# Decoder layer on one core: the first cross-attention batch loaded in 256 KB pieces, and self attention's loads and stores issued by ScalarE

## The reference

```python
x = x + self_attention(layernorm(x))       # 16 heads of 32, causal, biases
x = x + cross_attention(layernorm(x), ctx) # 16 query heads of 128 on 8 key/value heads; ctx is 64 tokens of 256, mask over them
x = x + experts(layernorm(x))              # 8 experts of rank 64; each token takes the expert of its largest logit
```

## Time and profile before

| | us |
|---|---|
| median of 3 runs | 1533.86 (1533.47 to 1535.66) |
| profiled execution | 1535.35 |
| its span, first to last instruction | 1533.6 |
| TensorE busy | 1382.5 (90% of the span) |
| VectorE / GpSimd / ScalarE busy | 1092.7 / 757.2 / 729.9 |
| mean granted TensorE clock | 0.966 |

### The profile page before, as it was taken

One profiled execution on the slowest core, in us unless ns is written; L12 is line 12 of the kernel. 1 busy time (PEld: TensorE's weight loads), 2 busy tenths in 40 slices (PEclk: granted clock), 3 DMA queues, 4 the chain that ended last, 5 costly groups with the idle time before them and its releaser, 6 DMA issues.

```text
span 1533.6 us, 28325 instructions
## 1 busy us (share of the span) xinstructions
PE 1382.5 (90%) x10592; PEld 1140.9 (74%) x10592; DVE 1092.7 (71%) x2037; ACT 729.9 (48%) x1739; POOL 757.2 (49%) x570
## 2 busy tenths in 40 slices
PE   7878778999998999999995778999999999999998
PEld 5656667777787877777874567888888887888886
DVE  4336486777878787877775577878787877787865
ACT  5444567666676667676674432323232323232221
POOL 2321266767777676867675643334343433343310
PEclk9999989999999999999998789999999999999999
DMA  8999587879898979888888731313130313030000
GB/s 321 306 316 292 118 153 135 166 159 160 169 162 160 164 141 182 162 168 168 155 145 232 189 144 47 116 34 125 30 138 28 133 33 132 28 136 30 28 15 28
DMA packets 378872, 212.57 MB, mean 139 GB/s; under 512 B 337648, under 2 KB 337776, under 8 KB 375024
## 3 DMA queue, kind: packets, MB, share of 16 engines
q1 hardware_dynamic: 378736, 210.74, 57.1%
HBM read 76.49 MB, written 50.33 MB: 83 GB/s over the span
## 4 chain that ended last, share of the span: by engine, by line
PE 48%; DVE 26%; issue 5%; ACT 4%; DMA 4%; POOL 2%; SPq 0%; DVEq 0%; ACTq 0%; POOLq 0%
PE banks L44 35%; DVE a_neg_max L803 4%; PE banks L936 4%; PE banks L1535 3%; DMA a_turned<-shared 3%; DVE b_xn L1378 2%; PE banks L970 2%; DVE a_y_sum L822 2%; DVE shared L812 2%; ACT a_probs L706 2%; PE banks L944 2%; DVE b_probs L1427 1%; PE banks L971 1%; DVE b_row_sum L1432 1%; DVE b_row_max L1425 1%
## 5 line engine op out<-in xcount | busy, mean ns | idle before, releaser
L626 POOL TENSOR_TENSOR shared<-a_probs,shared 128x768 f16<-128x768 f32 (+1 forms) x192 | 349.4, 1820 | 204.9 <-DVE shared L812 183.0
L706 ACT ACTIVATE a_probs<-banks,a_neg_max 128x128 f32<-128x128 f32 (+3 forms) x512 | 265.1, 531 | 210.9 <-DVE a_neg_max L803 184.0
L803 DVE TENSOR_REDUCE a_neg_max<-banks 128x2 f32<-128x256 f32 (+3 forms) x256 | 203.7, 818 | 115.4 <-PE banks L944 114.7
L1231 POOL TENSOR_TENSOR b_probs<-b_probs,b_row_scale 128x1024 f32<-128x1024 f32 x32 | 61.0, 1907 | 200.8 <-DVE b_row_scale L1437 200.8
L970 PE MATMUL banks<-a_v,a_turned 128*128 128x96 bf16 x1280 | 123.5, 212 | 32.3 <-DMA a_turned<-shared 25.8
L970 PEld LDWEIGHTS banks<-a_v,a_turned 128*128 128x128 f16 x1280 | 99.8, 100 | 65.5 <-issue 34.5
L1212 POOL TENSOR_TENSOR b_rstd<-b_var,b_minus_half 128x1 f32<-128x1 f32 x64 | 35.3, 551 | 189.4 <-DVE b_var L1373 189.4
L1304 ACT ACTIVATE b_probs<-b_probs 128x1024 f32<-128x1024 f32 x32 | 33.9, 1059 | 182.2 <-DVE b_probs L1427 182.2
L971 PE MATMUL banks<-a_v,a_turned 128*128 128x64 bf16 x1280 | 119.3, 196 | 0.0
L44 PE MATMUL banks<-a_xt_hi,w_qkv_hi 128*128 128x512 f32 x256 | 110.5, 432 | 6.5 <-DVE a_yt_lo L777 4.7
L706 ACT ACTIVATION_READ_ACCUMULATOR a_probs<-banks,a_neg_max 128x1 f32 x512 | 105.9, 207 | 0.0
(11 more groups left out here) (172 smaller groups left out, 3983.2 us busy)
## 6 DMA issues: line engine op xcount, KB each, us to landing
m_dram<-c_m_out SPq DMA_DIRECT2D x8, 2048.0 KB, 13.7
vw_dram<-shared SPq DMA_DIRECT2D x32, 512.0 KB, 8.3
b_vw_raw<-vw_dram SPq DMA_DIRECT2D x8, 2048.0 KB, 8.0
shared<-m_dram SPq DMA_DIRECT2D x7, 2048.0 KB, 8.4
c_w_raw<-w_group_dram SPq DMA_DIRECT2D x7, 1280.0 KB, 11.5
a_x_res<-x_dram SPq DMA_DIRECT2D x32, 256.0 KB, 3.5
x_dram<-a_x_res SPq DMA_DIRECT2D x32, 256.0 KB, 2.9
b_x<-x_dram SPq DMA_DIRECT2D x32, 256.0 KB, 2.7
```

Source lines behind the costliest of these rows:

```text
L626: nc.gpsimd.tensor_tensor(part(u, 1), probs[:, u % PROB_SLOTS, 0:2 * columns_of(u // 2)], part(u, 0), ALU.subtract).then_inc(parts_ready, 1)
L706: ins = nc.scalar.activation(probs[:, u % PROB_SLOTS, to:to + width], score[:, j, at:at + width], ACT.Exp, bias=neg_max[:, c:c + 1], accum ...
L803: ins = nc.vector.tensor_reduce(neg_max[:, c:c + 2], score[:, 2 * half:2 * half + 2, at:at + width], AX, ALU.max, negate=True)
L1231: nc.gpsimd.tensor_tensor(probs[:, :, :], probs[:, :, :], row_scale[:, :].unsqueeze(2).to_broadcast([P, XH, S]), ALU.mult).then_inc(probs_ ...
```

## The change

Three things are done. In self attention ScalarE issues `load_x`, `load_x_res` and `store_x1` at the end of its round, and SyncE's loop keeps only the transposes; the residual of the last batch is loaded by SyncE after the last transposes (`LAST_X_RES_AT` one round later), and the last four stores stay with SyncE. The loads of the first cross-attention batch are cut into 256 KB pieces: eight for M, one a round in rounds 84 to 91, into two buffers that lie where xn was and in free space; x1 tiles 0 and 1 and the mask in round 92; VW's first two pieces in round 94, all by ScalarE; VW's other six and x1 tiles 2 and 3 by SyncE after the last transposes. The head of the next stage is woven in earlier and shared differently: M is split by ScalarE in rounds 93 and 94, its low parts are made by GpSimd in rounds 94 and 95 and by VectorE at the end of round 95 and after it; three of VW's four low parts go from GpSimd to VectorE; the split of the expert weights moves behind tile 1's exponentials; and for tiles 2 and 3 TensorE makes its scores ahead of `turn_probs` of the tile before.

```diff
-    LAST_X_RES_AT = B * NR - 1
+    LAST_X_RES_AT = B * NR
...
+        INPUTS_FREE_AT = (B - 1) * NR
...
@@ self attention, sync
             for r in range(B * NR + 1):
                 for u in units_of(r - 1):
                     turn_parts(u)
-                for use in FILLED[2 * r - 2] + FILLED[2 * r - 1] if r else []:
-                    if use[1] == "o":
-                        store_x1(use[0], [use[2]])
-                if r in X_AT:
-                    load_x(*X_AT[r])
-                if r in X_RES_AT:
-                    load_x_res(*X_RES_AT[r])
                 if r == LAST_X_RES_AT:
                     for t in range(TT):
-                        load_x_res(B - 1, t)
-                if r == WEIGHTS_FREE_AT:
-
-                    sp.wait_ge(gemm_full, PROJECTED)
-                    sp.wait_ge(x1_stored, TT * 16)
-                    sp.wait_ge(vw_stored, XG * 64 + 64)
-                    next(then)
+                        load_last_x_res(B - 1, t)
+
+            sp.wait_ge(vw_stored, XG * 64 + 64)
+            next(then)
@@ self attention, gpsimd
-                if r == B * NR - 2:
+                if r in (B * NR - 2, B * NR - 1, B * NR):
                     next(then)
-                if r == B * NR:
-                    pool.wait_ge(parts_ready, 2 * B * NR)
-                    next(then)
-                if r == B * NR + 1:
-                    next(then)
+            pool.wait_ge(parts_ready, 2 * B * NR)
             next(then, None)
@@ self attention, scalar: the end of a round
-            next(then)
+                for use in FILLED[2 * r - 2] + FILLED[2 * r - 1] if r else []:
+                    if use[1] == "o":
+                        store_x1(use[0], use[2])
+                if r in X_AT:
+                    load_x(*X_AT[r])
+                if r in X_RES_AT:
+                    load_x_res(*X_RES_AT[r])
+                if r == INPUTS_FREE_AT:
+                    act.wait_ge(gemm_drained, drained((B - 1, "xt", KT - 1)))
+                if INPUTS_FREE_AT <= r < INPUTS_FREE_AT + XG:
+                    next(then)
+                if r == WEIGHTS_FREE_AT:
+                    act.wait_ge(gemm_full, PROJECTED)
+                    act.wait_ge(x1_stored, TT * 16)
+                if r >= WEIGHTS_FREE_AT:
+                    next(then)
@@ cross attention, sync
-        for t in range(TT):
-            load_x1((0, t, t))
-        sp.dma_start(mask_u8[:, :], mask.to_broadcast([P, B * S])).then_inc(small_loaded, 16)
-        sp.dma_start(m_first[:, :], m_dram[0].rearrange("p g m -> p (g m)")).then_inc(m_first_loaded, 16)
-        load_vw(0)
+        for g in range(2, XG):
+            load_vw_first(g)
+        load_x1((0, 2, 2))
+        load_x1((0, 3, 3))
         yield
         load_m(1)
-        sp.wait_ge(vw_lo_by_pool, len(VW_POOL))
-        sp.wait_ge(vw_lo_by_dve, len(VW_DVE))
+        sp.wait_ge(vw_first_lo_ready, CHUNKS)
@@ cross attention, gpsimd
-            if second:
-                we_low(0)
             if is_tile(b):
                 scale_probs(b * TT + t)
...
             if second:
+                we_low(0)
                 we_low(2)
...
         deviation(2, 0)
-        yield
         m_low(0, 0, 0)
+        yield
         m_low(0, 2, 0)
+        yield
         deviation(2, 1)
         yield
         vw_low(0, 0)
-        vw_low(0, 2)
-        yield
-        vw_low(0, 3)
@@ cross attention, scalar (in step, the split of the expert weights and that tile's split_m move behind the xt2 copy)
-        act.wait_ge(m_first_loaded, 16)
-        for c in range(CHUNKS):
-            split_m(0, c, 0)
+        for g in range(XG):
+            nc.scalar.dma_start(m_first[g // HALF][:, g % HALF, :], m_dram[0, :, g, :]).then_inc(m_first_loaded, 16)
+            yield
+        for t in range(2):
+            nc.scalar.dma_start(x1[:, t, :], x1_dram[0, t * P:(t + 1) * P, :]).then_inc(x1_loaded[t], 16)
+        nc.scalar.dma_start(mask_u8[:, :], mask.to_broadcast([P, B * S])).then_inc(small_loaded, 16)
+        yield
+        act.wait_ge(m_first_loaded, XG * 16)
+        split_m(0, 0, 0)
+        split_m(0, 1, 0)
+        yield
+        split_m(0, 2, 0)
+        split_m(0, 3, 0)
+        for g in range(2):
+            nc.scalar.dma_start(vw_raw[:, g * D:(g + 1) * D], vw_dram[0, :, g, :]).then_inc(vw_first_loaded, 16)
+        yield
         yield
         copy_hi(flat(xt2_hi), turn[0][:, :], xt2_full, 1, xt2_hi_ready)
         for c in range(CHUNKS):
             split_vw(0, c)
         copy_hi(flat(xt2_hi), turn[0][:, :], xt2_full, 2, xt2_hi_ready)
@@ cross attention, vector
+        m_low(1)
         normalise(2, x1[:, 0, :], 0)
         yield
-        m_low(1)
         m_low(3)
...
-        for c in VW_DVE:
+        for c in range(1, CHUNKS):
             vw_low(0, c)
@@ cross attention, tensor (step)
+            lead = isinstance(here, int) and 1 < here < TT
+            if lead:
+                make_scores(b, t, here, par)
             if done and not second:
-                turn_probs(done[2], here is not None)
+                turn_probs(done[2], here is not None and not lead)
...
-            if here is not None and not second:
+            if here is not None and not second and not lead:
                 make_scores(b, t, here, par)
```

More of the change, by code:

```diff
@@ L715, in parts_hi, with load_x, load_x_res, store_x1 @@
                 nc.scalar.activation(part(u, 0), probs[:, u % PROB_SLOTS, 0:2 * columns_of(u // 2)], ACT.Copy).then_inc(hi_by_act, 1)
+            def load_x(b, t):
+                if t == 0:
+                    act.wait_ge(gemm_drained, drained((b - 1, "xt", KT - 1)))
+                nc.scalar.dma_start(xn[:, t, :], x[b, t * P:(t + 1) * P, :]).then_inc(x_loaded[t], 16)
+            def load_x_res(b, t):
+                if b and t == 0:
+                    act.wait_ge(x1_stored, b * TT * 16)
+                nc.scalar.dma_start(x_res[:, t, :], x[b, t * P:(t + 1) * P, :]).then_inc(x_res_loaded[t], 16)
+            def store_x1(b, t):
+                act.wait_ge(gemm_drained, drained((b, "o", t)))
+                nc.scalar.dma_start(x1_dram[b, t * P:(t + 1) * P, :], x_res[:, t, :]).then_inc(x1_stored, 16)
             for use in AHEAD:
@@ L1014 @@
 PLACE = {
-    "m1_lo": 17536, "m0_hi": 33920, "m0_lo": 50304, "vw_raw": 66688, "xt2_hi": 84096, "xt2_lo": 86144, "xn2": 88192, "mask_u8": 90240,
-    "m_first": 91776, "pt_hi": 91776, "pt_lo": 95872, "probs": 99968, "xn3": 104064, "hidden": 106112,
+    "m1_lo": 17536, "m0_hi": 33920, "m0_lo": 50304, "vw_raw": 66688,
+    "m_first0": 83072, "probs": 84096, "hidden": 88192,
+    "x1": 91776, "xt2_hi": 99968, "xt2_lo": 102016, "xn2": 104064, "mask_u8": 106112, "xn3": 106112,
     "m1_hi": 108160, "vw_hi": 124544, "we_hi": 140928, "we_lo": 158336, "x2": 175744, "xt3_hi": 183936, "mask_add": 186496, "mask_f": 188544,
-    "vw_lo": 190592, "xt3_lo": 206976, "ht_hi": 209024, "ht_lo": 211072, "x1": 219712, "small": 227904, "end": 229368,
+    "vw_lo": 190592, "xt3_lo": 206976, "ht_hi": 209024, "ht_lo": 211072,
+    "m_first1": 219776, "pt_hi": 219776, "pt_lo": 223872, "small": 227968, "end": 229368,
 }
@@ L1052, in cross_attention_and_experts @@
     vw_raw = at("vw_raw", PLACE["vw_raw"], [P, KT * EW], F32)
-    m_first = at("m_first", PLACE["m_first"], [P, MW], F32)
+    m_first = [at(f"m_first{n}", PLACE[f"m_first{n}"], [P, HALF, KT * 2 * S], F32) for n in range(2)]
     m_hi, m_lo = ([at(f"m{p}_{n}", PLACE[f"m{p}_{n}"], [P, MW], F32R) for p in range(2)] for n in ("hi", "lo"))
@@ L1154, in is_second, with m_source @@
         return isinstance(n, int) and n == 1
+    def m_source(b, c):
+        if is_first(b):
+            return m_first[c // 2][:, c % 2 * 2:c % 2 * 2 + 2, :].rearrange("p g m -> p (g m)")
+        return m_raw[:, chunk(c)]
     def m_lo_count(b):
@@ L1263, in gpsimd @@
         deviation(2, 0)
+        m_low(0, 0, 0)
         yield
-        m_low(0, 0, 0)
         m_low(0, 2, 0)
+        yield
         deviation(2, 1)
@@ L1287, in split_m @@
                     act.wait_ge(score_full, (b - 1) * TT)
[L1288 to L1289 removed]
+            nc.scalar.activation(m_hi[par][:, chunk(c)], m_source(b, c), ACT.Copy).then_inc(m_hi_ready, 1)
         def split_vw(b, c):
[L1292 to L1293 removed]
+            if c == 0 and is_first(b):
+                act.wait_ge(vw_first_loaded, XG * 16)
+            elif c == 0:
+                act.wait_ge(vw_loaded, b * 16)
             if not (isinstance(b, int) and b == 0):
@@ L1317, in step @@
                 copy_hi(flat(xt3_hi), turn[2][:, :], xt3_full, gated[2] + 1, xt3_hi_ready)
-            if second:
-                act.wait_ge(we_loaded, 16)
-                for k in range(KT):
-                    nc.scalar.activation(we_hi[:, k, :], vw_raw[:, expert_rows(k)], ACT.Copy).then_inc(we_hi_ready, 1)
-            if is_tile(b) and is_tile(b + 1):
+            if is_tile(b) and is_tile(b + 1) and not second:
                 for c in M_BESIDE[t]:
@@ L1334, in step @@
```

(6 more changed lines are left out.)

32 lines of the change are left out of this document (14 added, 18 removed).

## The result

The kernel after took 1539.88 us (median of 12 runs), the kernel before 1534.57 beside it: ratio 1.0041, 95% interval 1.0025 to 1.0057, so some 6 us slower. Forecast was 1524.0, in 1514 to 1532, with a chance of 0.80 for faster. The profiled execution of after took 1539.42 us with a span of 1537.6, 4.0 over the span of before.

The account below looks back on a forecast made before the run. TensorE bounds both stages; their handover stalls on transposes queued behind 5 MB. Gains of 13.7, then 14.4, fell to 8.3 at VW, ended at 9.3, about 10 with the clock; self attention 0: 1535.35 to 1525.4 profiled, 1524 median, range 1514 to 1532.

Parts of the forecast that it names:

- The stall: Handover, round 95's scores: transposes no longer stand behind 5 MB, so scores start at 835.5 instead of 849.2, gain 13.7 us.
- VW's six pieces: Handover, before tile 1's scores: VW lands at about 862, tile 1 starts at 869.0, gain down to 8.3 us.
- Behind tile 1's scores: Later handover: TensorE no longer waits for GpSimd behind its VW low parts, about +1 us.
- The expert split: Handover: moving it behind the exponentials gives 0, since VectorE's row subtraction ended as late as ScalarE's split.
- The lead: Handover, tiles 2 and 3: scores ahead of `turn_probs`, bounds +2 to -3 us, taken as 0.
- The x1 tile behind VW: Handover: SyncE still issues batch 1's VW ahead of the next x1 tile, so that wait stays.
- clock's return: End of the handover: TensorE's clock returning adds a little, taking the gain from 9.3 to about 10 us.
- Self attention, taken as 0: Rounds 0 to 91: loads and stores issued by ScalarE lie in its gaps; bounds -5 and +8 us, cost 0.
- (a): Handover: VW's pieces land one after another, the last at 880, tile 1 18 us later: 1542 us; chance 0.03.
- (b): Self attention, rounds with two issues: ScalarE held 2.0 us an issue, 28 us in all, 1552 us; chance 0.06.
- (c): Handover: VW lands at 868, or GpSimd's and VectorE's low parts hold each other: 1531 us; chance 0.17.
- (d): Handover: the VW wait does not appear and VectorE drops its contention, 14.4 us stay: 1517 us; chance 0.14.

Follow-up runs that it names:

- the run with the burst on ScalarE: Kernel before, with round 92's 5 MB (x1, mask, M, VW) issued in whole loads by ScalarE at the round's end instead of by SyncE: ratio 0.9982.
- VW by ScalarE: Kernel after, with VW's pieces 2 to 7 issued by ScalarE at the end of round 95 instead of by SyncE behind the residual loads: ratio 0.9976.
- combined: Kernel after, ScalarE issuing VW's pieces 2 to 7, tiles 2 and 3's scores behind turn_probs, expert-weight split put back, batch 1's first x1 before its VW: 1522.29 us.
- issues-only runs: Kernel before, with only self attention's x loads, residual loads and x1 stores (rounds 0 to 91) moved from SyncE to ScalarE, run twice: ratios 1.0018 and 1.0012.

## Why the prediction was wrong, point by point

The forecast was a gain of 10 us for the profiled execution, and it lost 4.0. Of these 14.0 us, 6.0 stand ahead of tile 1's scores (gain forecast 8.3, measured 2.3) and 8.0 behind them (forecast 1.7 more, measured 6.3 less).

*The stall: right in place, 1.5 us too large, and by the wrong cause.* Round 95 started at 836.98, forecast 835.5. The text put the stall down to the transposes' place behind 5 MB in SyncE's queue. The run with the burst on ScalarE shows that the place made 3.5 us of it and the 5 MB in flight 12.3. The forecast came near because the change took away both, and that is luck: by the same working a burst moved whole to another queue would have been given the same gain. The change helped because those bytes no longer flow at once. That they came in pieces is not enough: where ScalarE issues VW's last six pieces, 1.5 MB, together beside the last transposes, TensorE's waits for these between 836 and 862 us are 5.1 us (VW by ScalarE) and 9.1 (combined), in after 0.2:

```profile
PE banks L980 <- DMA a_turned<-shared: 5.1, 2, 4.0
...
PE banks L980 <- DMA a_turned<-shared: 9.1, 3, 4.5
```

All 5 MB in pieces at once were not tried. What remains of the bytes has its price by the same cause: the 12.2 us are 15.8 less in round 94, 1.3 more in round 93 beside the x1 and mask loads (7.1 to 7.6 us in all kernels made from after, 6.1 in before), 1.2 more in rounds 84 to 92 beside M's pieces, and 1.1 from ahead of these.

*VW's six pieces: the first failed term.* Forecast was VW at 862 and tile 1 at 869.0, a gain left of 8.3 us; it was 867.6 and 875.04, 2.3. The order was right, the length was not: GpSimd's last low parts ended at 854.2 instead of 850.2 (1.5 from round 95, 2.5 from 17.2 us after it instead of 14.7), the four residual loads and six pieces were issued by 861.9, 7.7 us after that against 6.4, and the rest took 13.1 against 12.4. 4.0 + 1.3 + 0.7 are the 6.0 us. Part of the 2.5 is GpSimd's two last low parts: they took 5.65 us (848.56), where one took 2.13 before, and VectorE's low part of M ran beside them (850.13, 2.08); that one held up the other was not tried. In the prediction's own working 852 + 9.2 is 861.2, taken as 862.

*Behind tile 1's scores: the second failed term, and the larger one.* Taken as +1 and 0, it was a loss of 4.6 at tile 3. Against before, the stretch from tile 1's scores to mask 1 changed by -0.3 us, the next one to mask 2 by +1.3, and the one to mask 3 by +3.6. The expert split was costed at 0 by VectorE's lateness; it cost 1.7, because both of VectorE's low parts now meet one of GpSimd's (3.46 and 3.62 us instead of 3.47 and 1.28). The lead's bounds of +2 and -3 were too narrow: it cost 3.9, because TensorE's scores, in part at the lower clock, now stand ahead of the transposes on which VectorE's order depends. The x1 tile behind VW stayed, as said. Another 1 to 2 us are lost behind tile 3 (end less mask 3: 592.9 before, 594.6 after, 593.3 to 594.6 in all kernels made from after, 592.2 to 592.9 in those made from before). That was not tried and stays open. The forecast's "clock's return", 0.7 us, has no row behind it; the mean granted clock between 820 and 850 us did rise, from 0.66 to 0.79, but no run shows what that gave back.

*Self attention, taken as 0:* the issues lie in gaps, as the waits of before and after show between 190 and 800 us (total, times, longest), and the issue of a load takes 0.33 to 0.45 us, that of a store 0.34 to 0.45 with one of 1.45 (ns, least, median, most):

```profile
ACT a_probs L687 <- DVE a_neg_max L813: 163.4, 112, 5.2
...
PE banks L980 <- DMA a_turned<-shared: 6.3, 7, 2.4
...
PE banks L946 <- ACT a_probs L687: 3.0, 3, 1.6
...
L706 ACTq DMA_DIRECT2D a_x_res<-x_dram x28: 334/334/452, 273.9 to 801.9; - x28
L710 ACTq DMA_DIRECT2D x_dram<-a_x_res x28: 338/350/1452, 316.8 to 835.8; - x28
```

They answer. The issue time fell, ScalarE's waits did not; the 2 us that the issues-only runs suggest are inside the bounds given. From round 0's scores to round 93's it took 1.7 us longer than before (649.24 against 647.58), most of it the 1.2 beside M's pieces.

*The rivals.* (a) fell: the pieces overlapped, issued within 3.1 us and landing 5.2 us (median) after their own issue:

```profile
b_vw_raw<-vw_dram SPq DMA_DIRECT2D x6, 256.0 KB, 5.2
```

The Trainium skill's page DMA: Bandwidth & Descriptors, section Rules for kernel authors, asks for at least 1 MiB per DMA; that did not decide here, and M in two loads of 1 MB at once was the slower way. (b) fell: ScalarE's issues had a median of 0.33 to 0.35 us, a quarter of the 1.4 that decides. Its own price was too low: two rounds a batch at 2.9 us are 5.8, not 4. (c), given 0.17, named much of what happened, VW at 868 and low parts on GpSimd and VectorE in each other's way, and priced it 9 us too low, without the lead. (d) fell.

The working that failed is the same in each place: links on the path behind the stall were priced once, by rows of before, and their bounds were not added up on the losing side (VW up to 870, 8 us; the lead 3; self attention 8).

## What to carry to other kernels

Where a transposing DMA stalls, ask how many bytes flow beside it before asking in which queue it stands. Here spreading the bytes over rounds ended the stall, and another issuer gave back 3.5 of its 15.8 us. When a late transfer is put behind an earlier one, look at everything that the engines' programs have behind its first use, since each engine passes the delay on in order: four small changes of order and issue were worth more here (19 us from after to the combined kernel, 7 of them a loss that stood in before too) than the end of the stall (12.2). Work that meets TensorE after idle time should be the work that others wait for. And where a forecast is a sum of links, add up their bounds too: the losing side here came to 19 us against a gain of 10.

## What was not expected of the hardware

- The issue of one transposing DMA held SyncE for 12.50 us while 5 MB from another queue were in flight; ScalarE had issued these in seven plain loads of 0.39 to 0.46 us each.
- Two 1 MB loads lengthened two rounds by 4.9 us, where eight pieces of the same bytes lengthened nine rounds by 1.5 to 1.9 (mean of eight profiles, against the two ways of loading there without M).
- A VectorE subtraction of two SBUF tiles that takes 1.28 us alone took 3.46 to 3.62 beside one of GpSimd's: it ended 1.15 us after GpSimd's did.
